# Last pass of a two-layer graph and mixture kernel: 8 output buffers for 4, 12 row buffers for 8, 3 weight buffers for 5

## The chip, the cores and the metric

The kernel runs on one core of a Trainium2 chip. The metric is the device time of one execution in microseconds (us). The core has engines that work side by side and wait for each other through semaphores: PE (TensorE, matrix products), ACT (ScalarE), DVE (VectorE), POOL (GpSimd) and SP (SyncE), which here only starts transfers.

## What is computed

The reference works on `x` of 128 graphs x 128 tokens x 128 features and applies four residual layers: graph attention, a mixture of 8 experts (two per token), graph attention again, and a mixture of 32 experts with one per token. The change touches only the last of them:

```python
def _L1_ffn_ref(x, router_w, router_b, W1, b1, W2, b2):
    xf = x.reshape(-1, D)                      # 16384 tokens, D = 128
    logits = xf @ router_w.T + router_b
    idx = jnp.argmax(logits, axis=-1)          # one of E = 32 experts
    w1t = jnp.take(W1, idx, axis=0)            # D x H, H = 32
    h = jnp.einsum('nd,ndh->nh', xf, w1t) + jnp.take(b1, idx, axis=0)
    h = jax.nn.relu(h)
    w2t = jnp.take(W2, idx, axis=0)            # H x D
    out = jnp.einsum('nh,nhd->nd', h, w2t) + jnp.take(b2, idx, axis=0)
    return jax.nn.relu(out).reshape(x.shape)
...
x = x + _L1_ffn_ref(_layernorm(x, axis=-1), ...)
```

## The kernel before

Each attention layer handles four graphs a step, chooses each token's expert, and scatters the token's row (128 features and four extra numbers: a statistic, the token's id) into a DRAM array `xs` that is sorted by expert and padded to tiles of 128 rows. A mixture layer then goes through this array tile by tile, each tile having one expert (or one pair), and scatters its results back by token id.

The last pass (from about 969 us on) is the second mixture. It has 160 tiles, taken four at a time as `QUADS` = 40 quads. Each engine has a loop of its own over the quads, written out in full; an engine does its instructions strictly in that order. For quad j:

- SP loads four tiles of rows from `xs` into `xq[j % NXQ]` (L373 to L379). From j = `NXQ` on it first waits until the outputs of quad j - `NXQ` have been stored (L376), since the residual and the ids are read from the same buffer.
- DVE scales the rows: `xnq` (L871).
- PE turns the four tiles over with four transposes (`turn`, recorded under L1044).
- ACT copies the result out of PSUM into `xnqT` (L988), before that copies the weights of four experts from the table `vt` into `vq[j % NVQ]` (L982), one copy of 161 columns a tile, and after that applies ReLU and bias to the first product: `hqT` (L995).
- PE computes the first product, 128 x 32 weights by 128 columns a tile (L1193), and the second, over 33 rows (L1183). An f32 product takes two instructions on PE, so each of these lines has eight a quad.
- DVE adds the residual: `oq[j % NOQ]` (L878), after waiting for the stores that last used this buffer (L877).
- POOL scatters the four tiles to the output by token id (L487), which counts up the semaphore `stored{j % NOQ}`.

The loops are staggered. In turn i PE does the transposes of quad i, then the second product of quad i - 2, then the first product of quad i. ACT in its turn i does the weight copies of quad i + 1, then `xnqT` of quad i, then `hqT` of quad i - 1. DVE does `xnq` of quad i, then `oq` of quad i - 2. `after(engine, name, n)` (L91) waits until the n-th event of a name has happened; the two that matter most here are ACT's wait before the weight copies, for the second product that last read the buffer, and PE's wait for `xnqT` before the first product:

```python
980:   after(act, "yq", j - NVQ)
981:   for q in range(4):
982:       last = act.activation(vq[j % NVQ][:, q, :], vflat[:, bass.ds(expert[...], VW)], ACT.Copy)
```

```python
1189:  after(pe, "vq", j)
1190:  after(pe, "xnqT", j)
1191:  after(pe, "hqT", j - 2)
```

Of the kernel before, what the change touches and what calls it, by code (L numbers as in the profile page):

```python
# [77 lines left out]
def program(nc, x, adj, W_0, a_0, gamma, beta, Wr, br, W1_0, b1_0, W2_0, b2_0,  # L78
            W_1, a_1, rw, rb, W1_1, b1_1, W2_1, b2_1, out):
    with ExitStack() as ctx:  # L80
        def sb(name, shape, dt=F32):
            return ctx.enter_context(nc.sbuf_tensor(name, shape, dt))
# [174 lines left out]
        YB = [bank[4][:, 0:2 * P], bank[5][:, 0:2 * P]]  # L257


        NXQ, NOQ, NVQ = 8, 4, 5  # L260
        xq = [sb(f"xq{s}", [P, G, ROW]) for s in range(NXQ)]
        xnq = sb("xnq", [P, G, P])
        xnqT = sb("xnqT", [P, T])
# [954 lines left out]
```

How the kernel before makes its waits and increments, by code:

```python
        def after(eng, name, n, per=1, k=None):  # L91
            if n >= 0:
                eng.wait_ge(sem(name), per * n + (per if k is None else k))
# [195 lines left out]
        @block.sync  # L290
# [9 lines left out]
            def fills(l, half):  # L300
                sp.wait_ge(sem("fill_row"), l + 1)
                for r in numbers(mybir.EngineType.SP, filli[l][0:1, 16 * half:min(16 * half + 16, NB[l])], DUMMY[l] - P):
                    sp.dma_start(xs[l][bass.ds(r, P), :], pad[:, :]).then_inc(sem(f"filled{l}"), 16)
# [1 line left out]
            def scattered(l):  # L305
                for s in range(NS):
                    uses = sum(1 for n in range((l + 1) * NG) if n % NS == s)
                    sp.wait_ge(sem(f"scattered{s}"), 16 * G * uses)
                sp.wait_ge(sem(f"filled{l}"), 16 * (NB[l] + 1))
# [16 lines left out]
            for n in range(2, NX):  # L327
                load(n)
            const("w2_in", w2s[:, :].rearrange("p (e c d) -> p (e c) d", e=E0, c=2), W2_0.rearrange("e (c p) d -> p (e c) d", c=2))
            const("b2_in", b2raw[:, :], b2_0.rearrange("(u e) d -> u (e d)", u=1).broadcast_to([96, E0 * P]))
            const("v_in", v1raw[:, :].rearrange("p (e h) -> p e h", e=E1), W1_1.rearrange("e d h -> d e h"))
            sp.wait_ge(sem("vt_zero"), 1)
            const("v2_in", vt[0:H1, :, H1 + 1:VW], W2_1.rearrange("e h d -> h e d"))
            const("v2_in", vt[H1:H1 + 1, :, H1 + 1:VW], b2_1.rearrange("(u e) d -> u e d", u=1))
# [664 lines left out]
        @block.tensor  # L999
        def _(pe):
            pe.wait_ge(sem("wraw"), 1)
            for l in range(2):
```

## Time and profile before

| | us |
|---|---|
| median of 3 runs | 1242.21 |
| lowest and highest run | 1237.01, 1242.61 |
| the profiled execution | 1237.54 |
| its span, first to last instruction | 1235.6 |
| busy in the span: PE / weight loads of PE | 975.4 / 863.4 |
| busy in the span: DVE / ACT / POOL | 724.1 / 726.1 / 775.7 |
| mean granted TensorE clock | 0.845 |

The first attention layer fills about the first 300 us, the first mixture the stretch from 345 to 670, the second attention layer reaches to about 890, and the last pass runs from 969 to the end. Times in the rows below are us from the start of the span unless marked ns. A row of a list of waits names who waited, for whom, the total, the number of times and the longest. "remote" or "another core or an unknown queue" means that the profile found no instruction that ended the wait; there is no other core here. "issue" means that it saw no wait. Starts of PE's instructions are recorded, their ends are modelled. "x8" in a row of the order of time means that eight instructions in a row are drawn together. The granted clock is a share of 2.4 GHz; only 0.5 and 1.0 occur as levels.

### The profile page before, as it was taken

What the parts mean: (1) busy time and instruction counts of PE and PEld (TensorE: products, weight loads), DVE (VectorE), ACT (ScalarE), POOL (GpSimd) and SP (SyncE); (2) the same over time, 40 slices, a digit from 0 to 9 for tenths busy, and PEclk for the clock granted to TensorE, in tenths of its full rate; (3) what the DMA queues carried; (4) which work ended last, traced back from release to release, by engine and by line L of the source; (5) the groups of instructions that cost most, each with busy time, mean ns of one, the idle gap of its engine ahead of it and who ended that gap; (6) DMA issues with size and microseconds to landing.
All of it is one profiled execution on the core that took longest, in us unless ns stands there. A gap on an engine that the chain in (4) does not pass through costs nothing.

```text
span 1235.6 us, 27195 instructions
## 1 busy us (share of the span) xinstructions
PE 975.4 (79%) x7093; PEld 863.4 (70%) x7093; DVE 724.1 (59%) x3251; ACT 726.1 (59%) x2408; POOL 775.7 (63%) x950
## 2 busy tenths in 40 slices
PE   5888988883079999999999489999982477767763
PEld 4677877772079999999999378888871355545542
DVE  4898999997136666666666158888884122222221
ACT  3989999881035555555555299999970333344431
POOL 3255588778626666667677316778787166666666
PEclk9989899985579999999999799999995556675665
DMA  8133322112266667766665212323212422222220
GB/s 196 57 99 121 122 87 71 58 36 62 79 174 181 189 181 189 183 187 185 178 183 145 61 27 65 86 73 86 75 41 81 117 81 83 76 80 80 81 63 10
DMA packets 146324, 130.72 MB, mean 106 GB/s; under 512 B 26434, under 2 KB 117420, under 8 KB 146176
## 3 DMA queue, kind: packets, MB, share of 16 engines
q1 hardware_dynamic: 123872, 92.89, 29.0%
q0 software_dynamic: 18272, 34.21, 8.2%
q10 hardware_dynamic: 4032, 1.89, 0.5%
q8 instruction: 63, 1.03, 0.4%
q14 instruction: 85, 0.70, 0.2%
HBM read 83.15 MB, written 49.61 MB: 107 GB/s over the span
## 4 chain that ended last, share of the span: by engine, by line
PE 49%; issue 20%; DVE 14%; another core or an unknown queue 7%; SPq 3%; ACT 3%; POOL 2%; DMA 1%; POOLq 0%; DVEq 0%; ACTq 0%
PE bank L1167 12%; PE bank L1152 11%; PE bank L1044 6%; PE bank L1183 4%; PE bank L1061 3%; SPq L303 2%; PE bank L1073 2%; PE bank L1193 2%; PE bank L1074 2%; PE bank L1085 2%; DVE pm L613 1%; PE bank L1164 1%; PE bank L1110 1%; DVE xnq L871 1%
## 5 line engine op out<-in xcount | busy, mean ns | idle before, releaser
L453 POOL DMA_INDIRECT xs<-staged,dst x256 | 259.0, 1012 | 84.3 <-issue 67.7
L967 ACT ACTIVATE hT<-bank,wt 128x128 f32<-128x128 f32 x620 | 177.3, 369 | 171.0 <-PE bank L1167 89.2
L487 POOL DMA_INDIRECT out<-oq,xq x160 | 161.4, 1009 | 109.3 <-DVE oq L878 65.8
L480 POOL DMA_INDIRECT x2d<-ob,xi x155 | 157.4, 1015 | 87.3 <-POOL ob L477 60.9
L1167 PE MATMUL bank<-w2s,hT 128*128 x1240 | 189.7, 289 | 0.0
L1152 PE MATMUL bank<-xnT,wt 128*128 128x128 f32 x1240 | 166.4, 278 | 0.4 <-ACT hT L967 0.4
L1167 PEld LDWEIGHTS bank<-w2s,hT 128*128 128x128 f32 x1240 | 163.3, 192 | 3.9 <-issue 0.2
L1152 PEld LDWEIGHTS bank<-xnT,wt 128*128 128x128 f32 x1240 | 153.0, 194 | 0.7 <-issue 0.6
L878 DVE SCALAR_TENSOR_TENSOR oq<-bank,xq 128x512 f32<-128x512 f32 x40 | 27.7, 692 | 194.8 <-remote 105.6
L840 DVE COPY xnT<-bank 128x128 f32<-128x128 f32 x155 | 45.2, 292 | 114.6 <-PE bank L1144 74.0
L988 ACT ACTIVATE xnqT<-bank 128x512 f32<-128x512 f32 x40 | 23.9, 597 | 147.7 <-remote 64.4
L916 ACT ACTIVATE p<-bank,nm 128x128 f32<-128x128 f32 x256 | 102.9, 402 | 12.9 <-DVE nm L638 11.6
L917 ACT ACTIVATE p<-bank,nm 128x128 f32<-128x128 f32 x256 | 104.7, 409 | 0.0
L1193 PE MATMUL bank<-xnqT,vq 128*32 128x128 f32 x320 | 69.4, 391 | 42.4 <-issue 40.8
L930 ACT ACTIVATE rl<-bank,rinv 128x128 f32<-128x128 f32 x256 | 97.2, 453 | 3.4 <-DVE staged L630 1.8
L428 POOL TENSOR_TENSOR ve<-mv,eps 128x4 f32<-128x4 f32 (+1 forms) x69 | 18.5, 268 | 125.3 <-DVE mv L513 124.2
L1085 PEld LDWEIGHTS bank<-hg,pt 128*128 128x128 f32 x512 | 68.6, 196 | 28.7 <-issue 28.7
L1193 PEld LDWEIGHTS bank<-xnqT,vq 128*32 128x32 f32 x320 | 46.1, 156 | 57.5 <-issue 49.7
L613 DVE SCALAR_TENSOR_TENSOR pm<-p 128x128 f32<-128x128 f32 x256 | 59.9, 289 | 39.7 <-ACT p L917 32.1
L1061 PE MATMUL bank<-wcat,xT 128*128 128x128 f32 x512 | 76.1, 297 | 4.3 <-ACT xT L905 4.3
L1044 PE MATMUL bank<-ident,xnq 128*128 128x128 f32 x160 | 42.8, 419 | 46.3 <-DVE xnq L871 45.9
L1073 PEld LDWEIGHTS bank<-wa,xT 128*128 128x128 f32 x512 | 73.0, 206 | 5.3 <-issue 2.0
(208 smaller groups left out, 2372.7 us busy)
## 6 DMA issues: line engine op xcount, KB each, us to landing
wt<-wpd SPq DMA_DIRECT2D x155, 258.0 KB
xq<-xs SPq DMA_DIRECT2D x160, 66.0 KB
xi<-xs SPq DMA_DIRECT2D x155, 66.0 KB
xb<-x2d SPq DMA_DIRECT2D x32, 258.0 KB
xb<-in_x SPq DMA_DIRECT2D x32, 256.0 KB
wpd<-w1c SPq DMA_DIRECT2D x56, 129.0 KB
xs<-staged,dst POOLq DMA_INDIRECT x256
out<-oq,xq POOLq DMA_INDIRECT x160
```

Source lines behind the costliest of these rows:

```text
L453: pool.indirect_dma_start(out=xs[l], out_offset=bass.IndirectOffsetOnAxis(ap=dst[b % ND][:, c:c + 1], axis=0), in_=stag[s][:, q, 0:ROW], i ...
L480: pool.indirect_dma_start(out=x2d, out_offset=bass.IndirectOffsetOnAxis(ap=xi[t % NXI][:, ID:ID + 1].bitcast(U32), axis=0), in_=ob[:, t % ...
L487: pool.indirect_dma_start(out=orow, out_offset=bass.IndirectOffsetOnAxis(ap=xq[j % NXQ][:, q, ID:ID + 1].bitcast(U32), axis=0), in_=oq[j % ...
L916: act.activation(p1[:, q, :], S[:, q, :], ACT.Exp, bias=nm[:, q:q + 1])
L917: last = act.activation(p2[:, q, :], S[:, q, :], ACT.Exp, bias=nm[:, q:q + 1], scale=SLOPE[l])
L967: last = act.activation(hT[t % 2][:, j, :], HID[t % 2][:, j, :], ACT.Gelu, bias=wt[t % NW][:, c:c + 1])
L1044: last = pe.transpose(to[:, q * P:(q + 1) * P], src[:, q, 0:P], ident[:, :])
L1061: last = pe.matmul(HB[:, c], xT[:, c], wcat[l][:, :], start=(q == 0), stop=(q == G - 1), skip_group_check=True)
L1073: pe.matmul(S[:, c], xT[:, c], wa1[l][:, :], start=False, stop=False, skip_group_check=True)
L1152: last = pe.matmul(HID[t % 2][:, j, :], wt[t % NW][:, c:c + P], xnT[t % 2][:, :], start=(j == 0), stop=(j == 3), skip_group_check=True)
L1167: last = pe.matmul(to, hT[t % 2][:, 2 * h + c, :], w2s[:, bass.ds(e + c * P, P)], start=False, stop=(h == 1 and c == 1), skip_group_check= ...
L1193: last = pe.matmul(HQ[j % 2][0:H1, q * P:(q + 1) * P], vq[j % NVQ][:, q, 0:H1], xnqT[:, q * P:(q + 1) * P], start=(q == 0), stop=(q == 3), ...
```

## The change

Three numbers change, in one line. Nothing is added to the loops and nothing moved. All places that use the numbers follow: the modulo of the buffers, the distance of SP's wait (L376), of DVE's wait for a free output buffer (L877), of ACT's wait for a free weight buffer (L980), and the names of the semaphores that go with the buffers.

```diff
@@ -257,7 +257,7 @@
         YB = [bank[4][:, 0:2 * P], bank[5][:, 0:2 * P]]
 
 
-        NXQ, NOQ, NVQ = 8, 4, 5
+        NXQ, NOQ, NVQ = 12, 8, 3
         xq = [sb(f"xq{s}", [P, G, ROW]) for s in range(NXQ)]
         xnq = sb("xnq", [P, G, P])
         xnqT = sb("xnqT", [P, T])
```

## Rows read from the trace of the kernel before

**Rows 1.** Stage table: stretch, its length, busy us of each engine, clock, DMA.
```profile
350.00:640.00 290.00, 289.64 (x2555) 284.72 (x2555) 182.06 (x802) 154.31 (x540) 191.39 (x260) 0.99 0.69 185
...
985.00:1003.00 18.00, 15.32 (x64) 11.39 (x62) 3.94 (x7) 7.48 (x27) 11.78 (x12) 0.50 0.33 91
...
985.00:1231.00 246.00, 165.58 (x759) 126.02 (x757) 48.57 (x76) 91.61 (x329) 161.39 (x160) 0.60 0.25 72
```

**Rows 2.** POOL's scatters: count, shortest/median/longest ns, first and last start.
```profile
L487 POOL DMA_INDIRECT out<-oq,xq x160: 982/984/1352, 985.3 to 1229.8; - x160
```

**Rows 3.** Waits from 970 to 1236: total us, times, longest.
```profile
POOL out L487 <- DVE oq L878: 65.8, 19, 25.2
...
DVE oq L878 <- remote: 105.6, 14, 9.0
...
DVE xnq L871 <- DMA xq<-xs: 21.7, 2, 20.3
```

**Rows 4.** Order of time, undisturbed: start, us, engine, line, tiles, [idle before <- releaser].
```profile
1032.78 1.91 PE L1193 MATMUL bank<-xnqT,vq 128*32 128x128 f32 x8
...
1034.63 1.12 PE L1044 MATMUL bank<-ident,xnq 128*128 128x128 f32 x4
...
1035.67 2.07 PE L1183 MATMUL bank<-vq,hqT 33*128 33x128 f32 x8
1035.78 0.60 ACT L988 ACTIVATE xnqT<-bank 128x512 f32<-128x512 f32 x1 [2.40 <-PE bank L1044]
...
1037.28 1.00 ACT L982 ACTIVATE vq<-vt 128x161 f32 x4
...
1037.68 1.91 PE L1193 MATMUL bank<-xnqT,vq 128*32 128x128 f32 x8
```

**Rows 5.** Order of time, around one late stretch.
```profile
1026.00 0.98 POOL L487 DMA_INDIRECT out<-oq,xq  x1 [0.30 <-issue]
...
1029.87 0.98 POOL L487 DMA_INDIRECT out<-oq,xq  x1 [2.89 <-DVE oq L878]
...
1039.52 1.12 PE L1044 MATMUL bank<-ident,xnq 128*128 128x128 f32 x4
...
1040.57 1.16 PE L1183 MATMUL bank<-vq,hqT 33*128 33x128 f32 x8
...
1044.37 0.98 POOL L487 DMA_INDIRECT out<-oq,xq  x1 [0.30 <-issue]
1045.59 0.60 ACT L988 ACTIVATE xnqT<-bank 128x512 f32<-128x512 f32 x1 [7.31 <-remote]
...
1046.28 1.89 PE L1193 MATMUL bank<-xnqT,vq 128*32 128x128 f32 x8 [4.55 <-issue]
...
1047.14 0.69 DVE L878 SCALAR_TENSOR_TENSOR oq<-bank,xq 128x512 f32<-128x512 f32 x1 [8.06 <-remote]
...
1048.62 0.98 POOL L487 DMA_INDIRECT out<-oq,xq  x1 [3.27 <-DVE oq L878]
```

**Rows 6.** Order of time, PE at the upper clock level.
```profile
1055.46 1.06 PE L1193 MATMUL bank<-xnqT,vq 128*32 128x128 f32 x8
...
1056.91 0.66 PE L1044 MATMUL bank<-ident,xnq 128*128 128x128 f32 x4 [0.39 <-DVE xnq L871]
...
1057.50 1.16 PE L1183 MATMUL bank<-vq,hqT 33*128 33x128 f32 x8
```

**Rows 7.** Order of time, start and end of the last pass.
```profile
981.67 2.07 PE L1183 MATMUL bank<-vq,hqT 33*128 33x128 f32 x8
...
985.28 1.00 POOL L487 DMA_INDIRECT out<-oq,xq  x1 [25.24 <-DVE oq L878]
...
1229.75 0.98 POOL L487 DMA_INDIRECT out<-oq,xq  x1 [0.30 <-issue]
```

**Rows 8.** Order of time, POOL in the first mixture.
```profile
453.22 1.04 POOL L480 DMA_INDIRECT x2d<-ob,xi  x1 [0.79 <-POOL ob L477]
...
457.45 1.04 POOL L480 DMA_INDIRECT x2d<-ob,xi  x1 [0.79 <-POOL ob L477]
```

## The prediction

> **What bounds the kernel now.** I first read the stage table, to see what the last pass is worth. From 985 to 1231 us it occupies 246 us; POOL is busy for 161.39 of them, PE (TensorE) for 165.58, ACT and DVE for far less, at a mean granted clock of 0.60 [rows 1]. No engine is full by that count, so what matters is which engine waits for which. POOL's 160 scatters are the closest thing to a bound: a scatter lasts 984 ns [rows 2], and with the 0.30 us that the engine shows between two of them [rows 5] one costs 1.29 us and a quad of four tiles 5.16 us. Forty quads are 206.4 us, and some thirteen of the 160 scatters last about 0.3 us longer, which makes 210.5. POOL runs from 985.28 to 1230.73 [rows 7], 245.5 us. So it stands still for 35 us, in some thirteen pauses of about 3 us, each after eight or twelve scatters in a row.
>
> The second view is the waits of this stretch. DVE's longest are 105.6 us before the final addition (L878), 14 times, released by something that the profile can't name; ACT has waits of the same kind before L988. POOL waits 65.8 us for L878, of which 25.2 is the start of the pass. For rows from DRAM DVE waits only twice in the whole pass [rows 3].
>
> The third view is the order of time. An undisturbed turn goes round in 4.90 us: the second product (L1193) starts at 1032.78 and again at 1037.68. PE goes from L1193 to the four transposes (L1044) after 1.85 us, from there to the output product (L1183) after 1.04, and that takes 2.07. ACT's transposed copy (L988) runs under L1183. Its four weight copies (L982, 1.00 us) run at 1037.28, before L1183 has ended; they are for the quad two ahead, and nothing waits for them [rows 4]. PE has no idle time in such a turn, and it is a shade faster than POOL (4.90 against 5.16).
>
> A disturbed turn looks different. POOL has scattered without a pause since 1029.87. PE's transposes stand at 1039.52, end by the record at 1040.64, and ACT, free since 1038.28, reads their result only at 1045.59. DVE's L878 follows at 1047.14, although L1183 stands at 1040.57 in the trace. POOL's last scatter of the burst ended at 1045.35, so both are freed around its end, and POOL, out of work, resumes at 1048.62 [rows 5]. Thirteen of the pauses look alike: results of PE reach others late from 7 to 8 us into a burst of scatters on, and arrive 0.2 to 1.8 us after the burst is over. This lateness, and not a buffer, makes POOL's pauses.
>
> **The change part by part.** *Eight output buffers for four.* L878 for quad 10, at 1047.14, needs the stores of quad 6. The last of those scatters started at 1026.00 [rows 5], twenty us before. Over the 36 quads that have such a wait the distance is nowhere under twelve. Price now and then: nothing. A quad's producer turn, 4.90, is too near to POOL's 5.16 for a queue of more than three finished quads to form before the next late stretch.
>
> At this point a rule speaks for the change. The Trainium skill (Perfetto Trace Analysis, Optimization Strategy) says that a gap which repeats on the engine that ought to be full can mean too few buffers. POOL's pauses are such a pattern, and by the rule the 35 us would be won. The rows of L878 speak against it, because the buffer was free each time; I keep it as a rival.
>
> *Twelve row buffers for eight.* The wait for loaded rows occurs only at the start, before a first load has landed [rows 3]; loads stay ahead. SP's queue now waits for quad j-12 where it waited for j-8. Twelve quads instead of eight are loaded unhindered at the start. Price zero; at worst the four extra loads lie beside the first scatters, and a load that is delayed has 13 us or more to spare.
>
> *Three weight buffers for five.* This is the part that costs. ACT fills buffer (i+1) mod 3 in its turn i, and so must wait until L1183 has used quad i-2. That product is issued by PE in turn i, behind the transposes. Before, the wait was for quad i-4, long done. Behind it on ACT's queue stand the transposed copy (L988) of the same turn, and PE's L1193 needs that. So what ran under L1183 now comes after it. From the end of L1183: 0.15 until the first copy (a release of ACT by PE takes 0.03, from the end of the transposes at 1035.75 to 1035.78 [rows 4], rounded to 0.05, and the copy's address is a register operation behind the wait, estimated 0.10); 0.92 for four copies until the next instruction starts (1.00 for the group, less an overlap of some 0.1 [rows 4]); 0.60 for L988 [rows 4]; 0.10 from its end to L1193 (1046.19 to 1046.28 [rows 5]). Together 1.77. Then 1.85 + 1.04 + 2.07 as before. A turn is 6.73 us against 4.90. DVE's two operations, 1.4 us after the end of L1183, end before PE reaches the transposes, so they add nothing.
>
> The sum: the first L1183 ends at 983.74 [rows 7] in either kernel, since ACT's new wait there begins with it. The wait exists up to the copy for quad 39, so the next 37 ends come 6.73 us apart: 983.74 + 249.0 = 1232.8 for quad 37. POOL starts 1.54 us after it, L878 between them, as from 983.74 to 985.28 now [rows 7]: 1234.3. It is free then, since 5.16 is less than 6.73. Quads 38 and 39 come without the wait, faster than POOL takes them, so 3 x 5.16 = 15.5 gives 1249.8. From the last scatter's end to the span's end it is 4.9 now (1230.73 to 1235.6): 1254.7, and 1.9 lies around the span (1237.54 less 1235.6): 1256.6.
>
> Two terms are open. *The late stretches.* With the wait POOL scatters four times, 5.16 us, and then pauses 1.57. Lateness began 7 us or more into a burst. In the first mixture POOL issues two scatters each 4.23 us (453.22 to 457.45) with a pause of 0.79 before each pair [rows 8], and PE is busy 289.64 of 290 us there [rows 1]: short bursts with short pauses did no harm. So I take zero. The upper bound is today's loss carried over: 245.5/40 = 6.14 a turn against 4.90, 1.24 us, times 37 = 46. *The clock.* All of the turn above is at the lower level, 1.2 GHz. At the upper one (1055.46 to 1058.66) L1193 takes 1.06, the transposes 0.59 to the next start, and L1183 1.16 [rows 6]: a turn would be 1.77 + 1.00 + 0.59 + 1.16 = 4.52. The clock was 0.60 over the pass, so a fifth of it at 2.4 GHz. In the new turn PE stands idle 1.8 of 6.7 us, which it doesn't in an undisturbed turn now. Between 0.50 and 0.60 the gain is 0 to 37 x 2.2 x 0.2 = 16; I take 2, as PE does less per us. That gives 1254.6. The profiled execution, 1237.54, lies 4.7 under the median of 1242.21, at the low end of the runs; I set 1255.
>
> **Rivals.**
> - *As forecast, with late stretches on top.* For it: I can't name what delays PE's results, and POOL stays at 77% of the time. Against it: the mixture. All of today's loss gives 1256.6 + 46 = 1303, half of it 1280.
> - *The clock makes it up.* If the upper level is granted for a fifth to a quarter of the pass as now, 1257 - 16 to - 20 = 1237 to 1241, no measurable change.
> - *Faster by the clock.* The decisive point is a mean turn of 6.14. Below it the new kernel wins, which takes over 27% of the time at 2.4 GHz. With half of the turns there the mean is 5.6, and 37 x 1.1 = 42 less gives 1215. For it: short gaps may be too short to lower the clock. Against it: the clock stayed at 0.50 for the first 18 us after 985, with PE busy for 15.32 of them [rows 1].
> - *The outputs do what they seem to.* POOL never pauses: 985.3 + 210.5 + 4.9 + 1.9 = 1203. It needs ACT's new wait to be hidden too, and the order of the instructions excludes that at the lower clock.
>
> **How the numbers follow.** Forecast case (1245 to 1265) 0.55; with late stretches 0.17; clock makes it up 0.15; faster by the clock 0.09; pauses closed 0.04. The low end of the range, 1238, takes in most of the third case; the high end, 1282, half of today's late stretches. A measurement of this kernel can tell about 0.5% from no change, here 1236 to 1248. Faster is the last two cases, 0.13; no change is the third case and the forecast's low edge, 0.17; slower 0.70.
>
> **What would show it.** In the new profile ACT's L982 should wait for PE's L1183 some 37 times, about 1.7 us after L995 is done; starts of L878 should lie 6.7 us apart; POOL should show groups of four scatters with pauses of 1.5; the nameless waits before L878 and L988 should be gone; the clock should be 0.50 to 0.55; the last scatter should end near 1248. If nameless waits remain beside this pattern, the second case holds. If L878 comes in 5.2 us steps, the argument on ACT's wait is wrong. A clock of 0.60 or more makes it too slow a forecast.

## The result, and the profile after

The changed kernel takes 1251.95 us, the median of 6 runs (1249.33 to 1257.16); the kernel before takes 1238.99 beside it, also the median of 6 (1237.01 to 1242.61). The ratio is 1.0102, with a 95% interval of 1.0071 to 1.0134: slower by 1%. The profiled execution took 1252.77, with a span of 1250.7.

The waits of the last pass (965 to 1251 us), in the form of [rows 3]: who waited for whom, total us, times, longest.

```profile
DVE oq L878 <- PE bank L1183: 155.3, 31, 6.0
ACT vq L982 <- PE bank L1183: 112.3, 28, 4.8
POOL out L487 <- DVE oq L878: 77.4, 30, 24.8
ACT vq L982 <- issue: 69.8, 10, 33.4
```

The second row is new: ACT now waits for PE's second product before it copies weights. 28 of the waits are named, and nine of the ten under "issue" belong to them as well; the tenth, 33.4 us, is the start of the pass. The nameless waits of [rows 3] are gone, and with them the long bursts of scatters.

The stage table, in the form of [rows 1]: stretch, length, busy us of PE, PEld, DVE, ACT and POOL, clock, DMA share, GB/s.

```profile
985.00:989.00 4.00, 2.28 (x17) 1.91 (x17) 1.29 (x2) 2.50 (x9) 1.11 (x2) 0.93 0.47 114
989.00:1064.00 75.00, 55.36 (x226) 41.88 (x226) 14.18 (x22) 27.56 (x99) 44.87 (x46) 0.50 0.35 95
1064.00:1067.00 3.00, 1.28 (x12) 1.12 (x12) 1.29 (x2) 2.00 (x8) 1.80 (x3) 1.00 0.09 28
...
985.00:1246.00 261.00, 184.09 (x772) 140.04 (x771) 49.76 (x77) 95.12 (x342) 157.29 (x160) 0.53 0.25 69
```

PE's busy time rose from 165.58 us (759 recorded instructions) to 184.09 (772), mainly since the mean granted clock fell from 0.60 to 0.53: eight instructions of L1183 take 2.07 us at the lower level and 1.16 at the upper one. The upper level comes only in four short stretches, two of which stand in the table.

The order of time over one turn: start, us, engine, line, tiles, [idle before <- releaser].

```profile
1045.88 0.69 DVE L878 SCALAR_TENSOR_TENSOR oq<-bank,xq 128x512 f32<-128x512 f32 x1 [5.37 <-issue]
...
1050.42 2.07 PE L1183 MATMUL bank<-vq,hqT 33*128 33x128 f32 x8
...
1052.53 0.69 DVE L878 SCALAR_TENSOR_TENSOR oq<-bank,xq 128x512 f32<-128x512 f32 x1 [5.36 <-PE bank L1183]
1052.61 1.02 ACT L982 ACTIVATE vq<-vt 128x161 f32 x4 [4.16 <-PE bank L1183]
...
1053.53 0.57 ACT L988 ACTIVATE xnqT<-bank 128x512 f32<-128x512 f32 x1
...
1054.02 0.98 POOL L487 DMA_INDIRECT out<-oq,xq  x1 [1.81 <-DVE oq L878]
1054.21 1.89 PE L1193 MATMUL bank<-xnqT,vq 128*32 128x128 f32 x8 [1.72 <-ACT vq L982]
...
1056.03 1.12 PE L1044 MATMUL bank<-ident,xnq 128*128 128x128 f32 x4
1057.07 2.07 PE L1183 MATMUL bank<-vq,hqT 33*128 33x128 f32 x8
```

L1183 starts at 1050.42 and again at 1057.07, so a turn is 6.65 us where [rows 4] have 4.90. L982 starts 0.12 after the end of L1183, L988 0.92 later, and PE, idle for 1.72, begins L1193. In [rows 4] the same four copies and L988 lay under PE's work. POOL has been idle for 1.81 when the next quad comes. Over the pass it has 37 pauses of more than 0.6 us, 62.3 us together, where the kernel before has 14 with 39.9.

The last scatter:

```profile
1243.52 0.98 POOL L487 DMA_INDIRECT out<-oq,xq  x1 [0.31 <-issue]
```

It ends at 1244.50, and 6.2 us follow until the end of the span; before, it was 4.9.

### The profile page after: what moved, and what is told of

It reads as the page before. It is cut to its first block, busy times and chain, and to the rows that moved or that the text cites. A ratio compares the mean times of both kernels' runs of the same rounds, so it can differ in the third digit from the quotient of the medians.

```text
span 1250.7 us, 27193 instructions
## 1 busy us (share of the span) xinstructions
PE 991.7 (79%) x7093; PEld 874.8 (70%) x7093; DVE 724.1 (58%) x3251; ACT 725.9 (58%) x2408; POOL 769.5 (62%) x950
## 4 chain that ended last, share of the span: by engine, by line
PE 42%; issue 21%; POOL 13%; DVE 12%; ACT 5%; SPq 3%; DMA 2%; ACTq 1%; POOLq 0%; DVEq 0%
PE bank L1167 12%; PE bank L1152 11%; POOL xs L453 8%; PE bank L1183 4%; PE bank L1193 4%; PE bank L1044 3%; POOL staged L441 2%; SPq L303 2%; ACT vq L982 2%; PE bank L1164 1%; DVE stC L510 1%; PE bank L1144 1%; DVE pm L613 1%; PE bank L1061 1%; DVE nmax L637 1%
## 5 line engine op out<-in xcount | busy, mean ns | idle before, releaser
L487 POOL DMA_INDIRECT out<-oq,xq x160 | 157.3, 983 | 124.5 <-DVE oq L878 77.4
L982 ACT ACTIVATE vq<-vt 128x161 f32 x160 | 40.7, 326 | 182.2 <-PE bank L1183 112.3
L878 DVE SCALAR_TENSOR_TENSOR oq<-bank,xq 128x512 f32<-128x512 f32 x40 | 27.7, 692 | 202.6 <-PE bank L1183 155.3
L1193 PE MATMUL bank<-xnqT,vq 128*32 128x128 f32 x320 | 73.1, 407 | 65.8 <-ACT vq L982 55.7
L1193 PEld LDWEIGHTS bank<-xnqT,vq 128*32 128x32 f32 x320 | 48.3, 163 | 84.1 <-ACT vq L982 64.1
L1183 PE MATMUL bank<-vq,hqT 33*128 33x128 f32 x320 | 79.2, 423 | 0.0
L1183 PEld LDWEIGHTS bank<-vq,hqT 33*128 33x128 f32 x320 | 68.2, 313 | 12.9 <-issue 12.9
```

The lines of the kernel that those rows point to most:

```text
L487: pool.indirect_dma_start(out=orow, out_offset=bass.IndirectOffsetOnAxis(ap=xq[j % NXQ][:, q, ID:ID + 1].bitcast(U32), axis=0), in_=oq[j % ...
L1183: last = pe.matmul(YQ[j % 2][:, q * P:(q + 1) * P], hqT[j % 2][0:H1 + 1, q * P:(q + 1) * P], vq[j % NVQ][0:H1 + 1, q, H1 + 1:VW], start=(q ...
L1193: last = pe.matmul(HQ[j % 2][0:H1, q * P:(q + 1) * P], vq[j % NVQ][:, q, 0:H1], xnqT[:, q * P:(q + 1) * P], start=(q == 0), stop=(q == 3), ...
```

## The experiments

The kernel before was run again with each series, and takes 1189 us on two of three chips and 1241 on the third. Which chip the result above came from isn't recorded; the kernel before took 1239 there, with the nameless waits, so it behaves like the third. The theory of the prediction (A in the expectations) is that ACT's wait for a weight buffer puts 1.7 us of its work into PE's turn; rows and outputs cost nothing.

**Weights alone.** Only `NVQ` changes.

```diff
-        NXQ, NOQ, NVQ = 8, 4, 5
+        NXQ, NOQ, NVQ = 8, 4, 3
```

> Only the weight buffers go from 5 to 3; row and output buffers stay at 8 and 4. Theory A (ACT's wait for the second product makes the whole effect): the same as the changed kernel, ratio 1.008 to 1.014 to the kernel before, 1250 to 1254 us, with L878 every 6.65 us, single bursts of four scatters and no nameless wait before L878. Theory B (the deeper row and output buffers take part, for instance by keeping SP's loads out of the way): a different turn, over 7 us or with nameless waits, and above 1257 us.

On the first chip it took 1238.88 us against 1188.63, ratio 1.0408 (1.0367 to 1.0448). Its waits over the last pass:

```profile
DVE oq L878 <- PE bank L1183: 203.4, 40, 5.5
ACT vq L982 <- PE bank L1183: 149.6, 37, 4.2
POOL out L487 <- DVE oq L878: 80.5, 38, 20.0
```

ACT's wait for L1183 stands here 37 times by name. The starts of L878 are 6.65 us apart, and POOL has 37 pauses with 62.3 us, as in the changed kernel. The three weight buffers make the whole pattern alone. The ratio I had expected, 1.008 to 1.014, was missed. The miss lies outside the turn: on this chip the kernel before is 50 us faster than where I had made the forecast, and the stages ahead of the pass are 12 us shorter (POOL's first scatter at 975.0, against 987.6 in the changed kernel's profile).

**Rows and outputs alone.**

```diff
-        NXQ, NOQ, NVQ = 8, 4, 5
+        NXQ, NOQ, NVQ = 12, 8, 5
```

> Only the row buffers go from 8 to 12 and the output buffers from 4 to 8; the weight buffers stay at 5. Theory A: no difference, ratio 0.997 to 1.003, the same pauses of POOL after eight or twelve scatters and some 100 us of nameless waits before L878. Theory C (too few output buffers make POOL's pauses): POOL's pauses close, the ratio falls to 0.97 (about 1203 us).

1190.84 us, ratio 1.0020 (1.0003 to 1.0038), beside the same runs of the kernel before. Its waits:

```profile
DVE oq L878 <- DMA out<-oq,xq: 79.6, 20, 5.1
...
POOL out L487 <- issue: 47.6, 156, 0.3
...
POOL out L487 <- DVE oq L878: 18.4, 4, 17.4
```

POOL scatters without a pause, 0.3 us from one scatter to the next. DVE waits 20 times for a free output buffer and nobody suffers by it, since POOL has enough in stock. The pauses and nameless waits that I had expected here are absent in the kernel before on this chip too (see the second chip below), so this run says nothing on whether more output buffers would close such pauses. Of the 2 us more, 1.3 lie behind the last scatter: 6.2 us instead of 4.9.

**Four weight buffers.**

```diff
-        NXQ, NOQ, NVQ = 8, 4, 5
+        NXQ, NOQ, NVQ = 12, 8, 4
```

> Rows 12, outputs 8, weight buffers 4. ACT's copy then waits for the product of the quad before the one of the changed kernel, which has ended by then. Theory A: all of the loss is in the step from 4 to 3: the ratio is 0.997 to 1.003, turns of 4.9 us with late stretches as before. If the loss grew with every buffer taken away, it would be near 1.005.

1189.88 us, ratio 1.0014 (0.9997 to 1.0031). The step is between three and four. With four, ACT in its turn i waits for the product of quad i - 3, which PE issued a turn earlier, and hardly has to wait:

```profile
ACT vq L982 <- PE bank L1183: 7.5, 15, 0.5
```

POOL sets the pace on this chip with 5.2 us a quad, so equal times alone would only show that a turn of PE and ACT stays below that. The turns themselves show more: where nothing else holds PE up, L1193 starts again after 4.89 us at the lower clock level and after 3.12 at the upper one, as in the kernel before on the second chip.

**Three weight buffers, the transposed copy first.** The whole change, with one block of ACT's loop moved.

```diff
             for i in range(-1, QUADS + 1):
+                j = i
+                if 0 <= j < QUADS:
+                    after(act, "xq_ps", j)
+                    after(act, "hq_ps", j - 1)
+                    act.activation(xnqT[:, :], TQ[:, :], ACT.Copy).then_inc(sem("xnqT"), 1)
                 j = i + 1
...
                     last.then_inc(sem("vq"), 1)
-                j = i
-                if 0 <= j < QUADS:
-                    after(act, "xq_ps", j)
-                    after(act, "hq_ps", j - 1)
-                    act.activation(xnqT[:, :], TQ[:, :], ACT.Copy).then_inc(sem("xnqT"), 1)
```

> The changed kernel (12, 8, 3), but in each turn ACT does the transposed copy (L988) before the weight copies and their wait. Theory A (the harm is what stands behind the wait on ACT's queue, not the wait itself): L988 again runs under the second product, the turn is 4.9 us, the late stretches of the kernel before return, and the ratio is 0.997 to 1.004. Theory D (the wait costs wherever it stands, since the copies themselves come late for the next first product): a turn of 6 us or more and a ratio of 1.01.

1190.47 us, ratio 1.0019 (1.0004 to 1.0034). The waits, and the order of time around one of them; here L979 is the transposed copy and L987 the weight copies.

```profile
ACT vq L987 <- PE bank L1183: 41.8, 37, 1.5
```

```profile
1051.42 2.07 PE L1183 MATMUL bank<-vq,hqT 33*128 33x128 f32 x8
1051.53 0.60 ACT L979 ACTIVATE xnqT<-bank 128x512 f32<-128x512 f32 x1 [1.59 <-PE bank L1044]
...
1053.42 1.91 PE L1193 MATMUL bank<-xnqT,vq 128*32 128x128 f32 x8
1053.61 1.02 ACT L987 ACTIVATE vq<-vt 128x161 f32 x4 [1.49 <-PE bank L1183]
```

All 37 waits are still there, each as early as L1183 allows. But `xnqT` is already copied when ACT stands, and L1193 starts at 1053.42 without idle time. Undisturbed turns at the lower clock level are 4.89 us, as before. This is the sharpest test of A: at this level the wait by itself costs nothing; what is queued behind it does.

At the upper level the wait isn't quite free:

```profile
992.85 1.16 PE L1183 MATMUL bank<-vq,hqT 33*128 33x128 f32 x8
...
994.12 1.02 ACT L987 ACTIVATE vq<-vt 128x161 f32 x4 [0.78 <-PE bank L1183]
...
995.04 1.09 ACT L995 ACTIVATE hqT<-bank,vq 32x128 f32<-32x128 f32 x4
...
996.19 1.16 PE L1183 MATMUL bank<-vq,hqT 33*128 33x128 f32 x8
```

From L1183 to the copies, to `hqT` behind them and to the next L1183 it is 3.34 us, where the kernel before has 3.12 a turn. It doesn't show in the time, because POOL with 5.2 a quad is slower. Here too there were no late stretches to return, which A had expected for another chip.

**Both kernels on a second chip.** The kernel before and the changed kernel, as they are.

> The kernel before itself, for its profile beside the others of this series. If this chip is like the last one (1188.6 us): no nameless waits before L878 and L988, POOL scatters without a pause once it has started, 5.16 us a quad. If it is like the first (1237 us): pauses of 3 us after eight or twelve scatters.

> The changed kernel itself. Theory A: as with three weight buffers alone, ratio 1.041 where the kernel before takes 1188.6 us, 1.010 where it takes 1239; its own time hardly depends on the chip (1235 to 1252). Theory B (the deeper row and output buffers win something beside the new wait): a ratio under 1.035 on the faster chip.

The kernel before took 1188.97 us in its single run, and 1189.43 as the median of 7; the changed kernel 1240.03 (1236.45 to 1244.38), ratio 1.0434 (1.0395 to 1.0474). The waits of the kernel before on this chip, to be held against [rows 3]:

```profile
ACT xnqT L988 <- PE bank L1044: 102.3, 40, 10.5
DVE oq L878 <- DMA out<-oq,xq: 93.5, 23, 5.2
...
POOL out L487 <- issue: 46.1, 151, 0.3
...
POOL out L487 <- DVE oq L878: 22.9, 9, 20.5
```

No wait is nameless, and POOL has no pause: 208.5 us from its first scatter to the end of its last, 5.2 a quad. So the 35 us in which POOL stood still don't come with the kernel everywhere, and the same change costs 4.3% here and 1% where it was first timed.

**Is POOL the bound?** Two of four scatters are left out, so half of the output rows aren't written; the counts follow (L376, L382, L877).

```diff
-                for q in range(4):
+                for q in range(2):
```

> The kernel before with two of the four output scatters of each quad left out (half of the output rows are not written) and the counts of the waits for them halved. POOL's share of a turn falls to 2.58 us. Theory (POOL's scatters alone bound the pass before; the loop of PE and ACT has room): the pass shrinks to turns of 3.1 us, 1188.6 - 40 x 2.0 = 1108 us; on a chip with late results, these vanish too, since bursts of eight or twelve scatters don't occur. Rival (the loop of PE and ACT is near its own bound of 4.9): 1178 us.

1112.98 us, ratio 0.9363 (0.9330 to 0.9395). The stage table over its last pass:

```profile
960.00:1180.00 220.00, 114.83 (x800) 90.64 (x800) 51.83 (x80) 98.10 (x352) 78.63 (x80) 0.93 0.27 70
```

The window reaches beyond the end of the span, 1109.8; from 985 to 1095 us the clock is 1.00. Turns are 3.12 us. The kernel before has a clock of 0.60 from 985 to 1175 us on the same chip, and its undisturbed turns are 4.89 us at the lower level. So the other engines can take a quad in 3.12 us at 2.4 GHz and in 4.89 at 1.2 GHz, both less than POOL's 5.2, and it is POOL that sets the pace of the kernel before on a chip like this. It is a bound that the changed kernel, at 6.65, no longer touches.

**A pause on POOL before each quad.** A small operation on POOL, 0.75 us.

```diff
                 after(pool, "oq", j)
+                pool.tensor_tensor(rest[:, 2 * j:2 * j + 2], eps1[:, 0:2], neghalf[:, 0:2], ALU.pow)
```

> The kernel before with a small power operation (128 x 2) on POOL ahead of the scatters of each quad, which makes POOL pause for about 1 us after four scatters. On a chip where POOL scatters without pauses: slower by 40 x 1.0 = 40 us, 1228 (POOL is the bound). On a chip with late results: theory E (long bursts of scatters make PE's results late) gives turns of 6.2 us without late stretches and no change; theory F (the lateness comes from elsewhere) gives late stretches as before and more than 1250 us.

On the second chip, 1222.74 us, ratio 1.0286 (1.0251 to 1.0321): 39 pauses, 36.6 us in place of 39 x 0.3. I had expected 1228. POOL's time from first to last scatter grew by 31.4 us, to 239.9, and the whole by 33.3: where POOL is the bound, what it is given to do is paid.

**The chip with late stretches.** On a third chip the kernel before takes 1241.18 us (9 runs, 1238.73 to 1245.05). A profile of it there:

> The kernel before once more, in a third series: does this chip show the late stretches of the first trace (1237 us, nameless waits before L878 of some 100 us), or not, as two chips so far (1189 us, none)? Either way no other value between is expected.

1242.59 us in a single run. The nameless waits are back:

```profile
DVE oq L878 <- remote: 110.4, 14, 9.3
...
ACT xnqT L988 <- remote: 62.6, 9, 8.1
```

On this chip I tested the second theory (E): a long burst of scatters brings the lateness. The first test is three weight buffers with only two of the four weight copies from quad 3 on, so that half of the experts' weights are stale. It shortens POOL's pause from 1.81 to 1.35 us.

```diff
-        NXQ, NOQ, NVQ = 8, 4, 5
+        NXQ, NOQ, NVQ = 8, 4, 3
...
-                    for q in range(4):
+                    for q in range(4 if j < NVQ else 2):
```

> Row buffers 8, outputs 4, weight buffers 3, but ACT copies the weights of two tiles of a quad instead of four (the other two keep old weights, so half of the products use wrong ones). Theory A (the copies stand on the path of the turn): a turn is shorter by two copies of 0.23 us, 6.65 - 0.46 = 6.19 us, 38 x 0.46 = 17 us less than with three weight buffers and all copies: 1222 us on a chip where that took 1239. Rival (the copies lie beside other work and the turn is set by PE alone): 1239 us.

1241.56 us, ratio 0.9996 (0.9979 to 1.0014). A was right on the undisturbed turn, 6.20 us, 0.45 less for two copies, and the rival's 1239 is near the total by coincidence. I was wrong on the whole: I expected 1222, worked out from the first chip (1239 with all copies, first scatter at 975.0). Here the first scatter comes at 987.9, 13 us later, from the stages ahead; and POOL's pass takes 248.1 us, where 257.2 less 17 would be 240. These 8 us are lateness. Three weight buffers with all copies weren't run on this chip. In the order of time:

```profile
1032.43 0.98 POOL L487 DMA_INDIRECT out<-oq,xq  x1 [1.35 <-issue]
...
1038.63 0.98 POOL L487 DMA_INDIRECT out<-oq,xq  x1 [1.35 <-issue]
...
1043.92 0.98 POOL L487 DMA_INDIRECT out<-oq,xq  x1 [0.43 <-issue]
...
1047.78 0.99 POOL L487 DMA_INDIRECT out<-oq,xq  x1 [0.30 <-issue]
...
1050.07 0.69 DVE L878 SCALAR_TENSOR_TENSOR oq<-bank,xq 128x512 f32<-128x512 f32 x1 [6.35 <-remote]
1051.56 0.98 POOL L487 DMA_INDIRECT out<-oq,xq  x1 [2.79 <-DVE oq L878]
```

Groups of four scatters with 1.35 us between them do no harm. From 1041 to 1044 us, at a granted clock of 0.95, PE was faster, the pause shrank to 0.43 us, two quads became one burst of ten us (1038.63 to 1048.77), and the next result came late, 1.3 us after its end. DVE has seven such waits, 46.5 us, and each follows two or more quads with at most 0.7 us between them.

The second test is the pause before each quad again, on this chip.

> The kernel with a pause of about 1 us on POOL after each quad again, for the case that this chip shows late results in the kernel before. Then theory E (long bursts of scatters bring the lateness) expects 1240 us and no nameless waits, theory F (it comes from elsewhere) expects them with more than 1250 us. On a chip without late results it is 1223 us, as before.

1238.28 us in a single run, against 1241.18. Its waits, and one of POOL's turns (here L489 is the scatter, L487 the pause and L880 the final addition):

```profile
DVE oq L880 <- DMA out<-oq,xq: 138.0, 29, 5.2
...
POOL out L489 <- issue: 44.0, 160, 0.3
...
DVE oq L880 <- remote: 3.5, 1, 3.5
```

```profile
1086.16 0.98 POOL L489 DMA_INDIRECT out<-oq,xq  x1 [0.30 <-issue]
1087.14 0.75 POOL L487 TENSOR_TENSOR rest<-eps,neghalf 128x2 f32<-128x2 f32 x1
1088.08 1.04 POOL L489 DMA_INDIRECT out<-oq,xq  x1 [0.18 <-issue]
...
1093.21 0.76 POOL L487 TENSOR_TENSOR rest<-eps,neghalf 128x2 f32<-128x2 f32 x1
```

Of the 14 nameless waits of DVE, 110.4 us, one is left, 3.5 us. I had expected none. In the order of time nine results still reach ACT or DVE 0.4 to 1.7 us late, all before 1044 us; from there to the end none does. POOL does most quads in 6.08 us, about the mean turn of the kernel before with its lateness, 6.14: lateness is traded for pauses, and little is won. From the first scatter's start to the end of the last it is 239.6 us, against 247.9 in the profile of the kernel before on this chip. That 37 us of pauses don't lengthen the pass here, while they cost 2.9% on the second chip, supports E. In these pauses POOL isn't at rest, it works 0.75 us on something else; what they interrupt is the scatters. Whether it is the length of a burst or the number of scatters within some microseconds that counts, these kernels don't tell apart.

**A pause before every fifth scatter.**

```diff
                 for q in range(4):
+                    if (4 * j + q) % 5 == 0:
+                        s = (4 * j + q) // 5
+                        pool.tensor_tensor(rest[:, 2 * s:2 * s + 2], eps1[:, 0:2], neghalf[:, 0:2], ALU.pow)
```

> The kernel before with the small power operation on POOL only ahead of every fifth scatter. Bursts are then 5 scatters, 6.45 us, and a pause with its side costs is about 0.92 us, so a quad takes 5.16 + 0.74 = 5.9 us. Theory E (lateness needs bursts of 7 us and is taken back by a pause of 0.9 us): where the kernel before takes 1241 us, no nameless waits and 1241 - 40 x 0.24 = 1231 us, faster than both kernels; if bursts of 6.45 us are already too long, late stretches appear and the time is 1240 to 1260. On a chip without late results POOL is the bound, and the pauses cost 40 x 0.7 = 28 us: 1217 against 1189.

It ran on the first chip, which has no lateness: 1213.58 us against 1189.35, ratio 1.0204 (1.0181 to 1.0228), the price of 31 pauses; 1217 was expected. Whether it gains where results come late stays open. No version that writes the whole output was measurably faster than the kernel before on a chip where it ran.

## Why the prediction was right

**The turn.** Forecast 6.73 us, measured 6.65. Of its terms the copies and L988 cost 1.72 instead of 1.77 from the end of L1183 to L1193, L1193 to the transposes 1.82 instead of 1.85, and the rest is as in [rows 4]. The 0.10 for the copy's address stood in no row; the release and it together took 0.12, not 0.15. That the new wait would stand at the head of ACT's queue, with L988 behind it, is shown by three kernels: alone it makes the loss (weights alone), one buffer more removes it, and so does another order behind the same wait.

**The sum.** The forecast, before the 2 us for the clock, was a span of 1254.7. The changed kernel's span is 1250.7:

| term | forecast | measured |
|---|---|---|
| first L1183 of the 37 turns ends | 983.74 | 986.05 |
| 37 turns | 249.0 | 241.8 |
| from there to the end of the last scatter | 17.0 | 16.7 |
| last scatter to the end of the span | 4.9 | 6.2 |

The pass begins 2.3 us later, which lies in the stages ahead of it. The turns are shorter by 7.2: 37 x 0.08 = 3.0 by the size of a turn, and about 4 by the clock. The later start and the longer end, 3.6 together, hide half of that, so the total is nearer to the forecast than the turns are; that is luck, of a few us.

**The clock.** 0.53, in the forecast span of 0.50 to 0.55. The three later grants of the four shortened one turn each by 0.9 us and the next by 0.5: L878 comes after 5.74 and 6.12 us instead of 6.65. For the clock to make up the loss the mean turn had to be 6.2 to 6.3 us, and below 6.14 for a gain; it was 6.53.

**Late stretches.** Price zero, forecast and measured to within 1 us: no nameless wait in the changed kernel, in which four scatters alternate with 1.8 us without one. One result comes 0.6 us late, at 999.15, after two quads with 0.93 us between them. The reason given, bursts too short to bring lateness, is supported by the two tests on the third chip. Two readings behind it were off. In the first mixture 1.92 us lie between two pairs of scatters, not 0.79: POOL does two small operations there, and 0.79 is only its idle time, so the case is nearer to the new kernel's pause than I wrote. And the lateness doesn't begin as sharply as "7 to 8 us into a burst": in the burst from 1086.07 results that were due after 5.3 and 6.4 us are late, and four of ACT's late results arrive 1.4 us or more before POOL's pause instead of after the burst. I had not foreseen that the lateness isn't there on every chip. It decides the size of the loss. The pass of the changed kernel, first scatter to end of the last, takes 256.9 us where it was first timed (987.6 to 1244.5) and 257.2 for weights alone on the first chip (975.0 to 1232.2). It is bound by PE and ACT, and doesn't notice. The pass of the kernel before takes 245.5 with late stretches [rows 7] and 208.5 without. The forecast holds for the chip of the profile it was made from, where the loss is 13 us. On the second chip the changed kernel's 1240 us lies just inside the range, but the loss is 50 us there, since the kernel before is faster.

**Rows and outputs.** Price zero was mis-sized by about 2 us, of which 1.3 is behind the last scatter. It is 6.2 us in all five profiles with twelve row and eight output buffers and 4.9 in the eight with eight and four that scatter everything. In both cases SP sees the last store 1.2 us after the last scatter; what is longer is POOL's closing DRAIN instruction. The rival that more output buffers would close POOL's pauses wasn't tested: the kernel with rows and outputs alone ran only where POOL has no pauses, and the changed kernel has the new wait as well. Against it stands the argument of the prediction, which the trace of the kernel before bears out: over all 36 quads the last scatter that L878 needed had started 13.9 us or more before. The Trainium skill's rule (Perfetto Trace Analysis, Optimization Strategy), that a repeating gap can mean too few buffers, holds for the pauses of the changed kernel: they do come from too few buffers, those of the weights, three engines upstream of the gap.

## What to carry to other kernels

In this kernel cutting a buffer count was free until the wait it brought reached work of the same turn; then the price was all that is queued behind that wait and that someone needs, not the wait. Count, from the order of the loops, how many turns lie between a buffer's last reader and its next writer on an in-order queue (here 3 buffers cost 4.1% where POOL has no pauses, 1% where it has, and 4 nothing), and if memory is short, move what others need ahead of the wait. Before a stretch of idle time is used as a budget, see whether it is there on another chip.

## What the runs showed of the hardware

The same kernel is 4% apart on different chips, 1189 against 1241 us. One of them was used twice and gave 1188.6 and 1189.4. By the profiles of the kernel before, of the result and of the second chip, 12 us of the difference lie ahead of the last pass (POOL's first scatter at 973.5 and 985.3) and 37 in it. Where it is slow, results of PE that are due some 5 us or more into an unbroken burst of scatters reach ACT and DVE late, by up to 7.4 us, and in most cases within 2 us after the burst's end. In the profile on the third chip three results due 3.6 to 4.7 us into a burst were late too, by 1.0 to 2.5. With four scatters and then 0.93 us without one the late results shrank to nine, of at most 1.7 us, all in the first 52 us of the pass; two quads with 0.43 us between them brought a late one. Why only some chips do this isn't settled, nor what carries the delay.

With twelve row and eight output buffers the time after the last scatter is 1.3 us longer (6.2 for 4.9). It may hang on the eight semaphores that scatters then count up instead of four, but no run changes the outputs without the rows, and with half of the scatters and four semaphores it was 9.5 us, which I can't explain.
